# A gated-delta-rule layer with a mixture-of-experts gate on one core: weights loaded in the preparation, four buffers there, and the feed-forward loop written out with its first batch scaled late

## The reference

```
xn = layernorm(x)
s  = gated_delta_rule_layer(xn)           # 16 key heads, 32 value heads
g  = silu(ffn(xn))
out = x + s * g

def ffn(x):                               # x: 2048 tokens x 256
    probs = softmax(x @ W_router.T)       # 8 experts
    rw, sel = top_k(probs, 2)
    combine = zeros(T, 8).add(rw at sel)
    sh = (silu(x @ gate_s) * (x @ up_s)) @ down_s          # shared, inner width 704
    shared = sh * sigmoid(x @ W_sgate.T)
    h  = silu(x @ gate_e) * (x @ up_e)    # each of 8 experts, inner width 176
    return shared + sum_e combine[:, e] * (h_e @ down_e)
```

## Time and the profile before

| | us |
|---|---|
| median of 3 runs | 2868.14 (2868.12 to 2871.74) |
| the profiled execution | 2867.33 |
| its span, first to last instruction | 2865.60 |
| between its span and its time | 1.73 |
| preparation, to the first instruction behind its barrier | 102.06 |
| recurrent block, from about 500 | 2365.60 |

### The profile page before, as it was taken

How to read it: one execution, slowest core, us unless ns; L and a number is a source line. 1 busy time by engine, 2 the same in 40 slices (tenths; PEclk the granted TensorE clock), 3 DMA queues, 4 the chain that set the end, 5 groups by cost and what they waited for, 6 DMA issues and landing times.

```text
span 2865.6 us, 88023 instructions
## 1 busy us (share of the span) xinstructions
PE 2636.6 (92%) x34330; PEld 1955.6 (68%) x34330; DVE 2002.9 (70%) x4880; ACT 1621.1 (57%) x5068; POOL 1074.0 (37%) x1391
## 2 busy tenths in 40 slices
PE   3299999799999999999999999999999999999995
PEld 2155665577777777777777777777777777777774
DVE  3233222788888888778877888788878887788773
ACT  2111111566666666666666666666666666666662
POOL 0210220444444444444444444444444444444440
PEclk9799999899999999999999999999999999999997
DMA  1511220211121211111111111111111111111111
GB/s 43 164 39 24 62 62 1 73 42 57 42 57 42 57 49 49 49 49 49 49 49 49 49 49 49 49 49 49 49 49 49 49 49 49 49 49 49 49 49 62
DMA packets 225647, 146.87 MB, mean 51 GB/s; under 512 B 187457, under 2 KB 195937, under 8 KB 225121
## 3 DMA queue, kind: packets, MB, share of 16 engines
q1 hardware_dynamic: 219104, 123.58, 15.0%
q0 software_dynamic: 6144, 17.83, 2.6%
HBM read 115.81 MB, written 2.70 MB: 41 GB/s over the span
## 4 chain that ended last, share of the span: by engine, by line
PE 63%; DVE 9%; ACT 3%; issue 2%; DMA 2%; SPq 1%; POOL 1%; DVEq 0%; POOLq 0%; ACTq 0%
PE rps L811 11%; PE rps L736 8%; PE rps L744 7%; DVE conv L1264 6%; PE rps L698 4%; PE rps L828 4%; PE rps L715 3%; PE rps L867 3%; PE rps L858 3%; PE rps L682 3%; PE rps L841 3%; PE rps L776 2%; PE rps L785 2%; PE rps L708 2%; PE rps L685 2%
## 5 line engine op out<-in xcount | busy, mean ns | idle before, releaser
L1264 DVE SCALAR_TENSOR_TENSOR conv<-rps,w_in,conv 128x509 f32<-128x509 f32 (+2 forms) x768 | 571.9, 745 | 65.7 <-ACT conv L1052 47.6
L811 PE MATMUL rps<-xnT,w_in 128*128 128x512 f32 x1024 | 505.1, 616 | 13.5 <-DVE cols L1246 13.5
L1463 POOL TENSOR_TENSOR decay_b<-decay,beta_k 128x512 f32<-128x512 f32 x128 | 130.4, 1040 | 486.5 <-DVE beta_k L1280 486.5
L744 PE MATMUL rps<-w_z,xnT 128*128 128x256 f32 x1040 | 275.2, 388 | 0.9 <-ACT z L1001 0.7
L811 PEld LDWEIGHTS rps<-xnT,w_in 128*128 128x128 f32 x1024 | 174.7, 190 | 147.3 <-issue 123.9
L1414 POOL TENSOR_TENSOR o_t<-o_sq,q_mean 128x8 f32<-128x8 f32 x65 | 13.2, 204 | 688.6 <-ACT gated L985 688.6
L1052 ACT ACTIVATE conv<-rps,w_in 128x512 f32<-128x512 f32 x256 | 175.9, 687 | 163.2 <-PE rps L811 160.3
L736 PE MATMUL rps<-w_outn,gatedT 128*128 128x256 f32 x1056 | 241.4, 381 | 1.1 <-ACT gatedT L995 0.7
L441 DVE TENSOR_TENSOR silu_g<-fps_u,silu_g 128x512 f32<-128x512 f32 x68 | 47.0, 691 | 277.5 <-PE fps_u L460 127.7
L736 PEld LDWEIGHTS rps<-w_outn,gatedT 128*128 128x128 f32 x1056 | 201.7, 191 | 49.7 <-issue 23.8
L1066 ACT ACTIVATE qkT<-conv 128x512 f32<-128x512 f32 x128 | 80.6, 629 | 220.7 <-DVE conv L1264 220.7
(11 more groups left out here) (216 smaller groups left out, 6483.0 us busy)
## 6 DMA issues: line engine op xcount, KB each, us to landing
sums_row<-g_rows SPq DMA_DIRECT2D x65, 1024.0 KB, 5.0
scale<-comb_rows POOLq DMA_DIRECT2D x40, 256.0 KB, 5.4
w_in<-in_w_in SPq DMA_DIRECT2D x17, 520.0 KB, 3.5
bq<-bmat SPq DMA_DIRECT2D x256, 32.0 KB, 2.0
inv<-xq SPq DMA_DIRECT2D x256, 32.0 KB, 1.9
w_z<-in_w_z SPq DMA_DIRECT2D x17, 256.0 KB, 2.6
w_out<-in_w_out SPq DMA_DIRECT2D x17, 256.0 KB, 5.0
invT<-xqT SPq DMA_DIRECT2D x128, 32.0 KB, 2.1
```

Source lines behind the costliest of these rows:

```text
L744: last = nc.tensor.matmul(ps[Z_BANK[c // 2]][:, (c % 2) * D:(c % 2 + 1) * D], xnT[:, m, tb * T + c * C:tb * T + (c + 1) * C], w_z[:, m, :] ...
L811: last = nc.tensor.matmul(ps[PROJ_BANK[j]][:, :], w_in[:, m * 4 * P + j * P:m * 4 * P + (j + 1) * P], xnT[:, m, b * T:(b + 1) * T], start= ...
L1264: nc.vector.scalar_tensor_tensor(conv[:, j, shift:T], ps[PROJ_BANK[j]][:, 0:T - shift], w_in[:, k:k + 1], conv[:, j, shift:T], ALU.mult, A ...
L1463: nc.gpsimd.tensor_tensor(decay_b[:, us, :], decay[:, us, :], beta_k2[:, us].unsqueeze(2).to_broadcast([P, NC_, C]), ALU.mult).then_inc(db ...
```

## The change

The preparation's loop is written out for its 16 tiles on VectorE, ScalarE and TensorE, with four buffers (DEEP) for xn, ps_t and ps_s; ps_g shares banks with them. xt is gone: the projection reads xnT. VectorE normalises tile t before it copies the results of tile t - 3. TensorE waits for cst and ws alone (c_loaded). The tiles wg, wu and wd are allocated around both blocks, and SP issues their loads in the preparation. The feed-forward loop over batches is written out on every engine. In its first batch VectorE writes the first product into hid and multiplies by scale later: from column tile 8 (LATE) on, two tiles for each tile j. ScalarE there waits for the first product (prod_done), not for hid_done.

```diff
+DEEP = 4
+LATE = FT // 2
...
-        xn = sb("xn", [P, 2, D])
-        xt = sb("xt", [P, 2, D])
+        xn = sb("xn", [P, DEEP, D])
...
-        ps_g = [ctx.enter_context(nc.psum_tensor(f"ps_g{k}", [P, 512], F32)) for k in range(4)]
+        ps_g = ps_t[2:] + ps_s[2:]
...
+            for k, (j0, j1) in enumerate(GROUPS):
+                part = slice(j0 * P, j1 * P)
+                sp.dma_start(ffn["wg"][:, :, part], ffn["wg_dram"][:, :, part]).then_inc(ffn["w_in"][k], 16)
+                sp.dma_start(ffn["wu"][:, :, part], ffn["wu_dram"][:, :, part]).then_inc(ffn["w_in"][k], 16)
+            sp.dma_start(ffn["wd"][:, :, :], ffn["wd_dram"]).then_inc(ffn["wd_in"], 16)
...
-            with dve.Fori(0, BATCH) as b:
-                def normalise(c):
-                    k = c % 2
-
-                    dve.wait_ge(xnt_ps, b * NC_ + max(c - 1, 0) + BASE)
-                    nc.vector.tensor_scalar(xn[:, k, :], xs[:, bass.ds(b * NC_ + c, 1), :],
-                                            mean[:, bass.ds(b * NC_ + c, 1)], rstd[:, bass.ds(b * NC_ + c, 1)],
-                                            ALU.subtract, ALU.mult).then_inc(xn_ready, 1)
-
-                def take_small(c):
-                    k = c % 2
-
-                    dve.wait_ge(small_ps, b * NC_ + c + 1 + BASE)
-                    nc.vector.tensor_copy(a_bv[:, :, bass.ds(b, 1), :, c],
-                                          ps_s[k][:, 0:NV].rearrange("p (h o v) -> p h o v", v=REP, o=1)).then_inc(small_out, 1)
-                    nc.vector.tensor_copy(a_av[:, :, bass.ds(b, 1), :, c],
-                                          ps_s[k][:, NV:2 * NV].rearrange("p (h o v) -> p h o v", v=REP, o=1)).then_inc(small_out, 1)
-                    nc.vector.tensor_copy(routed[:, bass.ds(b * NC_ + c, 1), :],
-                                          ps_s[k][:, 2 * NV:NSMALL]).then_inc(small_out, 1)
-
-                normalise(0)
-                for c in range(NC_):
-                    if c < NC_ - 1:
-                        normalise(c + 1)
-                    take_small(c)
+            def normalise(t):
+
+                if t >= DEEP:
+                    dve.wait_ge(xnt_ps, t - DEEP + 1)
+                nc.vector.tensor_scalar(xn[:, t % DEEP, :], xs[:, t, :], mean[:, t:t + 1], rstd[:, t:t + 1],
+                                        ALU.subtract, ALU.mult).then_inc(xn_ready, 1)
+
+            def take_small(t):
+                b, c, k = t // NC_, t % NC_, t % DEEP
+
+                dve.wait_ge(small_ps, t + 1)
+                nc.vector.tensor_copy(a_bv[:, :, b:b + 1, :, c],
+                                      ps_s[k][:, 0:NV].rearrange("p (h o v) -> p h o v", v=REP, o=1)).then_inc(small_out, 1)
+                nc.vector.tensor_copy(a_av[:, :, b:b + 1, :, c],
+                                      ps_s[k][:, NV:2 * NV].rearrange("p (h o v) -> p h o v", v=REP, o=1)).then_inc(small_out, 1)
+                nc.vector.tensor_copy(routed[:, t:t + 1, :], ps_s[k][:, 2 * NV:NSMALL]).then_inc(small_out, 1)
+
+            for t in range(TILES + DEEP - 1):
+                if t < TILES:
+                    normalise(t)
+                if t >= DEEP - 1:
+                    take_small(t - DEEP + 1)
...
-            with act.Fori(0, BATCH) as b:
-                for c in range(NC_):
-                    k = c % 2
-                    act.wait_ge(xnt_ps, b * NC_ + c + 1 + BASE)
-
-                    act.wait_ge(small_ps, b * NC_ + max(c - 1, 0) + BASE)
-                    nc.scalar.activation(xt[:, k, :], ps_t[k][:, 0:D], ACT.Copy).then_inc(xt_ready, 1)
-                    nc.scalar.activation(xnT[:, :, bass.ds((b * NC_ + c) * P, P)],
-                                         ps_t[k][:, 0:D].rearrange("p (k t) -> p k t", k=KT), ACT.Copy).then_inc(xt_kept, 1)
+            for t in range(TILES):
+                act.wait_ge(xnt_ps, t + 1)
+                nc.scalar.activation(xnT[:, :, t * P:(t + 1) * P],
+                                     ps_t[t % DEEP][:, 0:D].rearrange("p (k t) -> p k t", k=KT), ACT.Copy).then_inc(xt_kept, 1)
...
-            with pe.Fori(0, BATCH) as b:
-                def transpose_tile(c):
-                    k = c % 2
-                    pe.wait_ge(xn_ready, b * NC_ + c + 1)
-
-                    pe.wait_ge(xt_kept, b * NC_ + max(c - 1, 0) + BASE)
-                    for m in range(KT):
-                        last = nc.tensor.transpose(ps_t[k][:, m * P:(m + 1) * P], xn[:, k, m * P:(m + 1) * P], ident)
-                    last.then_inc(xnt_ps, 1)
-
-                def project_small(c):
-                    k = c % 2
-                    pe.wait_ge(xt_ready, b * NC_ + c + 1)
-
-                    pe.wait_ge(small_out, TILES + 3 * (b * NC_ + max(c - 1, 0)))
-                    for m in range(KT):
-                        last = nc.tensor.matmul(ps_s[k][:, 0:NSMALL], xt[:, k, m * P:(m + 1) * P], ws[:, m, :],
-                                                start=(m == 0), stop=(m == KT - 1))
-                    last.then_inc(small_ps, 1)
-
-                transpose_tile(0)
-                for c in range(NC_):
-                    if c < NC_ - 1:
-                        transpose_tile(c + 1)
-                    project_small(c)
+            pe.wait_ge(c_loaded, 32)
+
+            def transpose_tile(t):
+                pe.wait_ge(xn_ready, t + 1)
+                if t >= DEEP:
+                    pe.wait_ge(xt_kept, t - DEEP + 1)
+                for m in range(KT):
+                    last = nc.tensor.transpose(ps_t[t % DEEP][:, m * P:(m + 1) * P], xn[:, t % DEEP, m * P:(m + 1) * P], ident)
+                last.then_inc(xnt_ps, 1)
+
+            def project_small(t):
+                pe.wait_ge(xt_kept, t + 1)
+                if t >= DEEP:
+                    pe.wait_ge(small_out, TILES + 3 * (t - DEEP + 1))
+                for m in range(KT):
+                    last = nc.tensor.matmul(ps_s[t % DEEP][:, 0:NSMALL], xnT[:, m, t * P:(t + 1) * P], ws[:, m, :],
+                                            start=(m == 0), stop=(m == KT - 1))
+                last.then_inc(small_ps, 1)
+
+            for t in range(TILES + 1):
+                if t < TILES:
+                    transpose_tile(t)
+                if t:
+                    project_small(t - 1)
...
-            with act.Fori(0, BATCH) as b:
+            for b in range(BATCH):
...
-                    act.wait_ge(hid_done, b * FT + max(j - 1, 0) + BASE)
+                    act.wait_ge(prod_done if b == 0 else hid_done, b * FT + max(j - 1, 0) + BASE)
...
             dve.sem_inc(prod_done, BASE)
             dve.sem_inc(hid_done, BASE)
-            with dve.Fori(0, BATCH) as b:
-
-                dve.wait_ge(scale_in, b * (16 * len(spans)) + 16 * len(spans))
+            for b in range(BATCH):
+
+                def scaled(j):
+                    dve.wait_ge(prod_done, b * FT + j + 1 + BASE)
+                    src = hid[:, j, :] if b == 0 else silu_g[:, j % 2, :]
+                    nc.vector.tensor_tensor(hid[:, j, :], src, scale[:, j, :], ALU.mult).then_inc(hid_done, 1)
+
+                if b:
+                    dve.wait_ge(scale_in, (b + 1) * 16 * len(spans))
                 for j in range(FT):
                     dve.wait_ge(silu_done, b * FT + j + 1 + BASE)
                     dve.wait_ge(u_ps, b * FT + j + 1)
                     if j == 0:
 
                         dve.wait_ge(o_ps, b * NC_ + BASE)
-                    nc.vector.tensor_tensor(silu_g[:, j % 2, :], ps_u[j % 2][:, :], silu_g[:, j % 2, :],
-                                            ALU.mult).then_inc(prod_done, 1)
-                    dve.wait_ge(prod_done, b * FT + j + 1 + BASE)
-                    nc.vector.tensor_tensor(hid[:, j, :], silu_g[:, j % 2, :], scale[:, j, :],
-                                            ALU.mult).then_inc(hid_done, 1)
+                    dst = hid[:, j, :] if b == 0 else silu_g[:, j % 2, :]
+                    nc.vector.tensor_tensor(dst, ps_u[j % 2][:, :], silu_g[:, j % 2, :], ALU.mult).then_inc(prod_done, 1)
+                    if b:
+                        scaled(j)
+                    elif j >= LATE:
+                        if j == LATE:
+                            dve.wait_ge(scale_in, 16 * len(spans))
+                        for q in (2 * (j - LATE), 2 * (j - LATE) + 1):
+                            if q < FT:
+                                scaled(q)
```

More of the change, by code:

```diff
@@ L389, in ffn_block @@
         ps_o = [ctx.enter_context(nc.psum_tensor(f"fps_o{k}", [P, 512], F32)) for k in range(2)]
-        w_in, wd_in, scale_in = [sem(f"ffn_w_in{k}") for k in range(len(GROUPS))], sem("wd_in"), sem("scale_in")
+        scale_in = sem("scale_in")
         g_ps, u_ps, silu_done, prod_done, hid_done = sem("g_ps"), sem("u_ps"), sem("silu_done"), sem("prod_done"), sem("hid_done")
```

52 lines of the change are left out of this document (24 added, 28 removed).

## The result

The changed kernel takes **2799.81 us**, the median of 4 runs (2797.58 to 2803.06), beside 2868.13 us of the kernel before on the same chip: ratio 0.9764, 95% interval 0.975 to 0.9778.

The account below looks back on a forecast made before the run. Hand-offs were taken to bound the preparation loop, and waits for weights and routing weights the first feed-forward batch. Gains 24.5 - 0.5 + 35.5 = 59.5 us gave 2808.6 us, range 2804 to 2813, wider range 2802 to 2817.

Parts of the forecast that it names:

- TensorE decides, 1.17 us: Preparation loop: TensorE's transposes and projection set the period at 1.17 us a tile, for a gain of 24.5 us.
- so I take the loop to run at 1.2 GHz: Preparation loop: TensorE assumed at the slow clock, since its 128x128 loads took 328 ns in the old loop.
- The rival: Preparation loop: clock rises inside the denser loop, twelve tiles at VectorE's 0.91 us, 3.1 us less, 2805.5; chance 0.10.
- hand-off bound, 0.83: Preparation loop: the way from a tile's transposes to its projection, 1.11 us, requires a period of at least 0.83 us.
- if the pace improves to VectorE's 0.91, 28.5: Preparation loop: upper bound of the gain, 28.5 us, if tiles ran at VectorE's 0.91 us.
- 0.5 later: Preparation start: weight loads issued early delay x, 0.5 us lost, bounds 0 and 2 us.
- The first batch: Feed-forward block: first batch shrinks from 98.6 to 63.1 us, gain 35.5 us, bounds 34 and 36.5.
- The routing weights: First feed-forward batch: landed 22.0 us after the barrier, first read at 34 us, cover 12 us.
- slow start: First feed-forward batch: a cold start of TensorE costing 2.1 us, held in the 55.3 us stretch.
- The written-out loops of the later batches: Feed-forward batches 1 to 3: writing out the loops gains 0, since TensorE showed no idle time at the turn.
- The early weights: Weights issued in the preparation: in by about 37 us, needed at 78, cover 40 us.
- the hand-offs' 1.7 us a tile: Preparation loop, rival: hand-off waits survive at 1.7 us a tile, 8 us lost, 2817; chance 0.08.

Follow-up runs that it names:

- e8: Changed kernel with nine extra 128x512 matmuls on TensorE ahead of the preparation loop, results unread; 2797.53 us.
- e1: Kernel before with only the changed preparation loop; weights still issued in the feed-forward block, whose batches loop and scale at once; 2837.00 us.
- e5: Changed kernel with the nine weight loads put back behind the barrier, into the feed-forward block; 2809.53 us.
- e7: Changed kernel with two buffers instead of four for xn, ps_t and ps_s, loop still written out; 2823.18 us.
- e10: Changed kernel with nine extra matmuls ahead of the loop, and the a_b copy moved from VectorE to ScalarE; 2801.58 us, a single run.
- the repeats: The changed kernel, unaltered, measured two more times; 2801.25 us and 2802.64 us.
- e6: Changed kernel with the first batch scaled at once like the others, VectorE waiting for scale before the first product; 2819.82 us.
- e4: The changed kernel measured again, unaltered; 2801.25 us.
- e12: Changed kernel with extra unread matmuls: ten ahead of the loop, twenty ahead of the sums, six behind the routing weights' transposes; 2798.15 us.
- e2: Kernel before with only the nine weight loads moved early, behind x in the preparation; 2849.97 us.
- e9: Changed kernel with extra unread matmuls: nine ahead of the loop, twenty ahead of the sums, six behind the routing weights' transposes; 2799.54 us.

## Why the prediction was wrong

**The step that failed** is "TensorE decides, 1.17 us", with "so I take the loop to run at 1.2 GHz" under it. 1.17 was right for the slow level: three tiles took 1.19. But the denser loop does not stay there. After some 6 us of the loop (5 to 8 in the other traces) the loads go from 0.97 to 0.52 us for four and the tile from 1.19 to 0.68. Eleven tiles from 28.75 to 36.44 take 7.7 us, and would take 13.1 at 1.19: 5.4 us of the miss. e8 shows that TensorE's work before sets the pace and its loads that this is the clock, e1 and e5 that no transfer has a part in it. In e7, with waits in each tile (2.23 us), the rise never came (333 ns a load throughout), as it never came in the loop before (2.64 us a tile).

**The rival had the mechanism and not its size.** It stood at 0.10 and 3.1 us, because it took VectorE's 0.91 us as the floor of the fast case. That was measured with register work in it, and written out VectorE needs 0.62. The prediction's hand-off bound, 0.83, did not hold either: it rests on 1.11 us from a tile's transposes to its projection at the slow clock, and at the fast one this took 0.97. That way sets the floor, 0.68 (rows in e10). So the bound "if the pace improves to VectorE's 0.91, 28.5" was no bound; the loop gave 30.2. The chance was too low for want of a row, and the range with it. The Trainium skill (TensorE: Matmul & The Clock Gate, Part 1) holds that sustained matmul work lifts the throttle; the loop's 0.97 to 0.52 us agrees. The Trainium skill's sentence in Part 4 of the same page, that transposes don't count as busy, was weighed against it, and must not be carried over to a loop in which a third of the matmuls are transposes: here the clock rose all the same. Whether the transposes had a share in that, no run here shows.

**The rest of the 8.8 us.** The first transposes came 0.14 us earlier than before, where 0.5 later was forecast: x did land later in this execution, by 0.23, and the stretch behind it was shorter (in the repeats the first transposes came at 22.63 and 22.66). With the 5.4 that makes most of the 6.2 us between 43.75 and 37.54. From a_a to the down-projection it took 96.9 us, forecast 97.4; from there to the recurrent block 0.35 us less than before. That is 7.1 us at the recurrent block's start (66.6 gained, 59.5 forecast). The block itself took 1.1 us more, the end 0.2, and the profiled execution was 2802.01, 5.8 below the forecast for it. The median lies 2.2 below that, where I had put it 0.8 above: 3.0 us, within the spread of the recurrent block (below). Without these 3.0 us the result would have been 2802.8, just inside the range, and of the two repeats one lies inside (2802.64) and one outside (2801.25). So the step that failed is clear of chance, and that the median fell outside the range is in part chance.

**What held.** The first batch: from the store of comb_rows to the down-projection the gain is 35.4 us (103.31 to 67.92), forecast 35.5. The routing weights came 24 us after POOL's first issue (e6: VectorE's wait ends at 96.54, issued from 72.43), forecast 21, and are first read 34.4 us after it: cover 10 us where I had 12. From the first matmul it took 62.9 us, forecast 62.2: 0.7 us more, nearly all of it slow start: the first column tile took 6.15 us (71.51 to 77.66), 2.7 more than the 3.43 of a later one, where 2.1 was forecast. The written-out loops of the later batches: 89.63 us a batch (134.43 to 224.06) against 89.57, no gain. The early weights: the last landed at 28.8, forecast 37. What they cost x was 0 to 0.3 us, at the low end of the 0 to 2: VectorE started at 9.89 here, but at 9.59 to 9.70 in seven other traces with early weights (e4, e6, e8 to e12), at 9.87 and 9.95 in e7 and e2, and at 9.60 to 9.66 in the four with late ones. And the hand-offs' 1.7 us a tile did not come: TensorE's waits in the loop were two, of 0.22 and 0.45 us, and the gaps of 0.10 us in the fast part.

## What to carry to other kernels

When a change closes the gaps of a stretch, ask again at which of TensorE's two clock levels it will run, and work the sum out for both: the price of every matmul in it may halve on the way. For the floor of the fast case take each engine's bare instructions, not a period that has loop registers in it, and go once round every hand-off with the durations of the fast clock. Two cures of one wait are worth about one; price the second on top of the first.

## What was not expected of the hardware

The granted-clock column did not show the rise. It reads 1.00 in all of the loop, at 0.97 us for four loads and at 0.52; the length of the loads told the level. Later it does follow. Windows of the changed kernel, two in the loop (slow and fast part), then one at the start of the feed-forward block, where a load takes 0.34 us, and one later in it, with one of its loads:

```profile
22.00:29.00 7.00, 6.04 (x29) 5.67 (x30) 3.65 (x19) 1.92 (x5) 0.32 (x1) 1.00 0.83 351
29.00:37.00 8.00, 7.93 (x69) 7.28 (x68) 6.76 (x44) 4.83 (x12) 0.00 (x0) 1.00 0.01 3
...
71.50:74.00 2.50, 2.49 (x3) 1.16 (x4) 0.00 (x0) 1.15 (x1) 2.35 (x4) 0.50 0.17 54
...
80.00:100.00 20.00, 20.00 (x48) 8.76 (x47) 4.15 (x6) 3.16 (x6) 7.88 (x12) 1.00 0.65 152
```

```profile
80.67 0.19 PEld L458 LDWEIGHTS fps_g<-xnT,wg 128*128 128x128 f32 x1 [0.24 <-issue]
```

So in a stretch near the program's start the loads are the better witness.

A gap of 2.25 us ahead of the loop (e9) was followed by a fall inside it, gaps of 1.06, 1.11 and 1.66 (e8, e12, e10) were not. At the barrier, gaps of 2.69 and 2.67 us were followed by a slow first group in e9 and a fast one in e12. What decides between these is not shown.

The recurrent block, the same code in all kernels, took 2347.3 (e1) to 2357.1 us (e5) from its first matmul to the end, at a granted clock of 0.99 in the changed kernel as before. In the traces of the changed kernel, e1 and e8 its 64 steps take 34.8 to 37.1 us each, growing over some seven to nine steps and falling back, at other steps in every execution. Differences of that size between executions are what hides the 2 to 7 us of e8, e9 and e12. Their cause stays open.
